# Sliding-window attention: the sum of each softmax row is formed by TensorE and applied to the output instead of to the weights

## The reference, cut to what matters

```
scores = einsum("bhncd,bhnkd->bhnck", qc, kc) * SCALE
scores = where(mask, scores, -inf)
attn = softmax(scores, axis=-1)
out = einsum("bhnck,bhnkd->bhncd", attn, vc)
return out.reshape(B, S, E) @ w_out.T
```

## Time and profile before

| | us |
|---|---|
| median of 3 runs | 731.71 |
| lowest and highest run | 730.83, 732.27 |
| the profiled execution, whole | 733.66 |
| its span, first to last instruction | 731.8 |
| PE, DVE, ACT, POOL busy | 653.5, 486.1, 435.4, 201.2 |

### The profile page before, as it was taken

The page is one execution under the profiler, slowest core; times in us unless marked ns, Lnnn a source line. Parts: engine busy times, 40 slices in busy tenths (PEclk is TensorE's granted clock), DMA queues, the critical chain, the costliest instruction groups (busy, mean ns, idle before and its releaser), DMA issues.

```text
span 731.8 us, 13912 instructions
## 1 busy us (share of the span) xinstructions
PE 653.5 (89%) x4832; PEld 535.8 (73%) x4833; DVE 486.1 (66%) x1091; ACT 435.4 (59%) x1124; POOL 201.2 (27%) x354
## 2 busy tenths in 40 slices
PE   7888788999998998978989999999978799999950
PEld 5666678999998998854567788888865388887840
DVE  2577676478488478458877856666556577777735
ACT  4997857357458358357878747465342366566612
POOL 2455421032000000010233434444126222222315
PEclk9999899999999999998999999999999999999985
DMA  8997000220220241410020000000195101111114
GB/s 287 387 326 223 1 1 1 91 91 1 91 91 0 91 124 83 134 39 1 1 87 1 2 1 2 1 1 1 64 428 200 58 30 52 49 50 50 51 59 135
DMA packets 32226, 62.03 MB, mean 85 GB/s; under 512 B 2500, under 2 KB 26824, under 8 KB 29928
## 3 DMA queue, kind: packets, MB, share of 16 engines
q1 hardware_dynamic: 30152, 56.04, 22.6%
q0 software_dynamic: 2016, 5.22, 2.0%
HBM read 45.80 MB, written 15.55 MB: 84 GB/s over the span
## 4 chain that ended last, share of the span: by engine, by line
PE 63%; ACT 15%; DVE 14%; DMA 3%; issue 3%; POOL 2%; SPq 1%; POOLq 0%; ACTq 0%; DVEq 0%
PE banks L1785 41%; PE bank L1785 22%; ACT arena L777 5%; DVE U_split L1254 4%; ACT U_split L796 2%; DVE mx L1208 1%; DVE arena L1345 1%; ACT arena L815 1%; DMA ys<-arena 1%; ACT arena L842 1%; DMA arena<-ys 1%; DMA cst<-in_cst 1%; DVE wabs L1368 1%; ACT xT L731 1%; ACT arena L951 1%
## 5 line engine op out<-in xcount | busy, mean ns | idle before, releaser
L1785 PE MATMUL banks<-U_split 128*128 128x512 f32 (+1 forms) x616 | 146.8, 350 | 6.1 <-DVE U_split L1254 4.0
L1785 PE MATMUL bank<-U_split 128*128 128x256 f32 (+1 forms) x864 | 112.1, 285 | 6.9 <-DVE U_split L1254 6.2
L1785 PEld LDWEIGHTS banks<-U_split 128*128 128x128 f32 x616 | 96.4, 190 | 23.8 <-issue 8.0
L1785 PEld LDWEIGHTS bank<-U_split 128*128 128x128 f32 x864 | 105.5, 189 | 10.8 <-DVE U_split L1254 6.5
L796 ACT ACTIVATE U_split<-arena 128x1024 fp32r (+6 forms) x122 | 96.9, 822 | 21.1 <-DVE arena L1345 9.4
L1785 PE MATMUL banks<-cst,arena 128*128 128x128 f32 (+1 forms) x594 | 90.5, 280 | 4.7 <-DMA arena<-xs 1.7
L1785 PE MATMUL banks<-arena 128*128 (+4 forms) x632 | 84.8, 382 | 3.3 <-DVE arena L1202 2.3
L1785 PEld LDWEIGHTS banks<-cst,arena 128*128 128x128 f32 (+1 forms) x594 | 69.9, 143 | 17.3 <-POOL arena L647 2.7
L571 POOL TENSOR_SCALAR rstd<-mv 128x1 f32<-128x1 f32 x38 | 10.7, 281 | 260.4 <-DVE mv L1186 236.4
L1785 PEld LDWEIGHTS banks<-arena 64*128 64x128 f32 (+3 forms) x632 | 61.3, 177 | 20.8 <-issue 7.5
L1044 ACT ACTIVATE arena<-banks,dmx 128x128 f32<-128x128 f32 (+1 forms) x128 | 52.9, 424 | 38.6 <-DVE dmx L1542 38.6
(11 more groups left out here) (239 smaller groups left out, 1180.1 us busy)
## 6 DMA issues: line engine op xcount, KB each, us to landing
arena<-in_w_exp SPq DMA_DIRECT2D x8, 1536.0 KB, 14.1
xs<-arena SPq DMA_DIRECT2D x8, 1032.0 KB, 13.8
arena<-in_ctxT SPq DMA_DIRECT2D x4, 1601.0 KB, 6.9
arena<-in_ctx SPq DMA_DIRECT2D x4, 1536.0 KB
arena<-in_w_f SPq DMA_DIRECT2D x3, 1024.0 KB, 11.5
arena<-xs SPq DMA_DIRECT2D x23, 129.0 KB, 2.0
w_x<-in_w_x SPq DMA_DIRECT2D x9, 256.0 KB, 7.0
arena<-in_w_oh SPq DMA_DIRECT2D x1, 2048.0 KB, 8.5
```

What stands on the lines that cost most here:

```text
L1785: return nc.tensor.matmul(o, w, x, start=start, stop=stop, **k)
```

## The change

Five things are changed, all in the first block and its neighbourhood.

1. The exponentials no longer keep a row sum (`accum_out` is gone); `rsum`, `rinv`, the reciprocal of 128x8 on DVE and the multiplication on POOL are gone. `a_transpose(n)` waits for the exponentials.
2. New on PE, `a_sums(n)`: eight products of the turned weights `PT` with constant columns (`halves`: ones in 16 of 32 columns), which give the row sums spread over the 16 output rows of each head, 128x128 per group. They go into free columns of PS[0] or PS[1] (in the last batch PS[6]). They stand ahead of `a_scores(n + 4)`; those of groups 12 to 15 stand after the loop's last scores.
3. New on DVE, `a_sum_inverse(n)`: the reciprocal of these 128x128 sums, from the bank into `oT`, in round n+4 between mask and max. `a_outT(b)` moves from ACT to DVE and multiplies PS[7] by `oT`. The scores of round n also wait for the inverse of round n-1.
4. `a_project_out(b-1)` moves on PE from behind the scores to behind the transposes of its round.
5. ACT copies the turned weights of three groups of four (i=0, 1, 2) instead of two, DVE those of one.

The counter `x_neg` is merged into `x_exp`, and the numbers of `const_set` move with the four new memsets of `halves`.

```diff
...
         def on_act(n):
 
-            return n % GROUPS in (1, 2)
+            return n % GROUPS != 3
...
-                pool.wait_ge(G["a_norm"], GROUPS * b + 1)
...
-                pool.wait_ge(G["a_rinv"], n + 1)
-                g.tensor_tensor(sm[:, n % 4, :, :], sm[:, n % 4, :, :],
-                                rinv[:, n % 4, :].unsqueeze(2).broadcast_to([P, H0F, P]), ALU.mult).then_inc(G["a_norm"], 1)
...
-                    a.activation(sm[:, n % 4, h, :], sm[:, n % 4, h, :], ACT.Exp, bias=mx[:, n % 4, h:h + 1],
-                                 accum_out=rsum[:, n % 4, h:h + 1]).then_inc(G["a_exp"], 1)
+                    a.activation(sm[:, n % 4, h, :], sm[:, n % 4, h, :], ACT.Exp,
+                                 bias=mx[:, n % 4, h:h + 1]).then_inc(G["a_exp"], 1)
...
-                    if b > 0:
-                        a_outT(b - 1)
...
+            def a_sum_inverse(n):
+                b, i = divmod(n, GROUPS)
+                f, t = divmod(i, TPB)
+                dve.wait_ge(G["a_z"], n + 1)
+                if i == 0 and b > 0:
+                    dve.wait_ge(G["a_y"], b)
+                v.reciprocal(oT[:, f, t * P:(t + 1) * P], sums_bank(n)).then_inc(G["a_zinv"], 1)
+
+            def a_outT(b):
+                dve.wait_ge(G["a_o"], b + 1)
+                dve.wait_ge(G["a_zinv"], GROUPS * (b + 1))
+                v.tensor_tensor(oT, PS[7][:, :].rearrange("p (k t) -> p k t", k=KT), oT, ALU.mult).then_inc(G["a_o_sb"], 1)
...
                 a_mask(n)
-                if n >= 1:
-                    a_rinv(n - 1)
+                if n >= 4:
+                    a_sum_inverse(n - 4)
                 a_max(n)
+                if i == 3 and b > 0:
+                    a_outT(b - 1)
...
+            dve.wait_ge(G["a_z"], NG - 1)
+            for n in range(NG - GROUPS, NG - 1):
+                a_sum_inverse(n)
             b_split_q(0)
             b_split_k(0)
             b_split_v(0)
             a_weightsT(NG - 1)
+            a_sum_inverse(NG - 1)
             for b in range(B):
+                if b == 0:
+                    a_outT(B - 1)
...
+            def a_sums(n):
+
+                b, i = divmod(n, GROUPS)
+                if n == 0:
+                    pe.wait_ge(G["const_set"], 8)
+                pe.wait_ge(*pt_done(n))
+                if b == B - 1:
+                    pe.wait_ge(G["xT_done"], B - 2)
+                    pe.wait_ge(G["a_zinv"], NG - GROUPS if n < NG - 1 else n)
+                o = sums_bank(n)
+                for j in range(2):
+                    for r in range(QUADS):
+                        ins = mm(o[r * D0P:(r + 1) * D0P, :], halves[:, j, :], PT[:, n % 2, 2 * r + j, :], start=j == 0, stop=j == 1,
+                                 tile_position=(0, r * D0P))
+                ins.then_inc(G["a_z"], 1)
+
...
                 if n > 0:
                     pe.wait_ge(G["a_add"], n)
+                if n >= 5:
+                    pe.wait_ge(G["a_zinv"], n - 4)
+                if n >= 4:
+                    a_sums(n - 4)
...
-                pe.wait_ge(G["a_norm"], n + 1)
+                pe.wait_ge(G["a_exp"], H0F * (n + 1))
...
-                if i == 3 and b > 0:
-                    a_project_out(b - 1)
...
                 if n >= 2:
                     a_transpose(n - 2)
+                if i == 3 and b > 0:
+                    a_project_out(b - 1)
...
```

More of the change, by code:

```diff
@@ L377, in build @@
             const_set ln_var ln_rstd ln_done xT_raw xT_done
-            a_q a_k a_v a_q_sb a_k_sb a_v_sb a_vmix a_s a_add a_max a_exp a_rinv a_norm
+            a_q a_k a_v a_q_sb a_k_sb a_v_sb a_vmix a_s a_add a_max a_exp a_z a_zinv
             a_pt a_pt_act a_pt_dve a_o a_o_sb a_y a_y_sb ld_rest
             b_q b_k b_v hi_part lo_part c_Thi c_Tlo c_Rhi c_Rlo wk_split b_s b_max b_exp b_t b_pt_hi b_pt b_o b_o_sb b_ot b_ot_sb b_y
-            x_k x_neg x_exp x_kf x_kf_hi x_kf_lo x_m1 x_m1_sb x_m1T x_m1T_sb x_kv x_kvbd
+            x_k x_exp x_kf x_kf_hi x_kf_lo x_m1 x_m1_sb x_m1T x_m1T_sb x_kv x_kvbd
             w_abs w_sum w_scale w_round w_tern
@@ L557, in _ @@
             g.memset(mhalf[:, :], -0.5).then_inc(G["const_set"], 1)
+            g.memset(halves[:, 0, 0:D0], 1.0).then_inc(G["const_set"], 1)
+            g.memset(halves[:, 0, D0:D0P], 0.0).then_inc(G["const_set"], 1)
+            g.memset(halves[:, 1, 0:D0], 0.0).then_inc(G["const_set"], 1)
+            g.memset(halves[:, 1, D0:D0P], 1.0).then_inc(G["const_set"], 1)
             pool.wait_ge(G["const_set"], 2)
@@ L757, in a_values @@
                              PS[6][:, :].rearrange("p (h c d) -> p h c d", c=2, d=D0), ACT.Copy).then_inc(G["a_v_sb"], 1)
-            def a_outT(b):
-                act.wait_ge(G["a_o"], b + 1)
-                if b > 0:
-                    act.wait_ge(G["a_y"], b)
-                a.activation(oT, PS[7][:, :].rearrange("p (k t) -> p k t", k=KT), ACT.Copy).then_inc(G["a_o_sb"], 1)
             def a_weightsT(n):
@@ L841, in x_exp @@
                 low = kf_lo[:, n % 3, 0:words]
-                a.activation(low, PS[KBANKS[c % 4]][:, 0:words], ACT.Relu, scale=-1.0).then_inc(G["x_neg"], 1)
-                act.wait_ge(G["x_neg"], n + 1)
+                a.activation(low, PS[KBANKS[c % 4]][:, 0:words], ACT.Relu, scale=-1.0).then_inc(G["x_exp"], 1)
+                act.wait_ge(G["x_exp"], 2 * n + 1)
                 a.activation(low, low, ACT.Exp, scale=-1.0).then_inc(G["x_exp"], 1)
@@ L876, in _ @@
                 if b == 0:
-                    a_outT(B - 1)
+                    act.wait_ge(G["a_o"], B)
                 x_exp(CP * b)
@@ L1026, in e_exp @@
                     act.wait_ge(G["e_qf"], b - 1)
-                a.activation(eq[:, b % 2, :], PS[QUERY_BANKS[b]][:, :], ACT.Relu, scale=-1.0).then_inc(G["x_neg"], 1)
-                act.wait_ge(G["x_neg"], CP * B + b + 1)
+                a.activation(eq[:, b % 2, :], PS[QUERY_BANKS[b]][:, :], ACT.Relu, scale=-1.0).then_inc(G["x_exp"], 1)
+                act.wait_ge(G["x_exp"], 2 * CP * B + b + 1)
                 a.activation(eq[:, b % 2, :], eq[:, b % 2, :], ACT.Exp, scale=-1.0).then_inc(G["e_exp"], 1)
@@ L1208, in a_max @@
                 v.tensor_reduce(mx[:, n % 4, :], sm[:, n % 4, :, :], AX, ALU.max, negate=True).then_inc(G["a_max"], 1)
-            def a_rinv(n):
-                dve.wait_ge(G["a_exp"], H0F * (n + 1))
-                v.reciprocal(rinv[:, n % 4, :], rsum[:, n % 4, :]).then_inc(G["a_rinv"], 1)
+            def a_sum_inverse(n):
+                b, i = divmod(n, GROUPS)
+                f, t = divmod(i, TPB)
+                dve.wait_ge(G["a_z"], n + 1)
[6 more added lines that the diff above has]
+                v.tensor_tensor(oT, PS[7][:, :].rearrange("p (k t) -> p k t", k=KT), oT, ALU.mult).then_inc(G["a_o_sb"], 1)
             def a_weightsT(n):
@@ L2116, in _ @@
                     to_xT(0, b - 2)
+                if n == NG:
+                    a_sums(n - 4)
                 if i == 0 and n > 0:
                     a_output(n - 4)
+                if n >= NG:
+                    a_sums(n - 3)
                 if n >= 3 and (n - 3) % GROUPS > 0:
```

20 lines of the change are left out of this document (11 added, 9 removed).

## The result

The changed kernel takes 739.19 us (median of 6 runs, 737.12 to 739.94), the kernel before beside it 731.99 us (6 runs, 729.4 to 734.74). The ratio is 1.0081, with a 95% interval of 1.0058 to 1.0104. The prediction said 738.7 us, with 731.5 to 743 as its range and a chance of 0.83 for slower. The profiled execution took 739.94 us with a span of 738.1 us, 6.3 us more than the span before.

A forecast was written before the change was run, and what follows sets the result against it. ACT was taken to bound the kernel, PE close behind. Full-clock stretches (about +4) and half clock (+3) on the profiled 733.66 us gave 740.7, or 738.7 us as a median; range 731.5 to 743.

The forecast's parts named there:

- ACT is late before, PE next: Kernel before, 11 to 96 us: row sums hang on ACT, busy 66.4 of 80.1 us; PE, busy 65.0, comes next.
- Exponentials, 1.6 us for eight: On ACT, eight exponentials without sums take 1.6 us instead of 3.1, saving ACT about 20 us of its 66.
- the two equations: Fit to ACT's copies from SBUF: 0.09 us per instruction plus 0.84 ns per column, giving 0.2 us for 128 columns.
- the first stretch: Scores of group 0 to those of 3: only the shorter exponentials act, -3.0 us.
- The inverse, 0.96 us: On DVE, a 128-column reciprocal takes 0.96 us from a slope of 6.3 ns per column; sixteen take 15.4 us.
- The projection rounds: Rounds n = 7, 11, 15: projection waits for DVE 3.83 us after scores; PE idles 1.5 to 3 us.
- The end: Scores of 15 to first cross scores: three inverses, 2.9 us, stand openly on the path; +3.5 us.
- The clock: PE drops to half clock behind gaps, about 1.5 us per stretch; two stretches taken, +3 us.
- A: Rival: PE's clock falls in all gaps, adding 5.5 to 8 us, taken as 742 us; chance 0.17.
- B: Rival: DVE's reciprocal is as cheap as other elementwise work, 0.3 us, taken as 732 us; chance 0.12.
- C: Rival: ACT was the only bound and PE runs dense, never waiting for multiplied outputs, 727 us; chance 0.06.
- D: Rival: ACT's exponentials keep their 390 ns pitch, so ACT gains nothing, 741.6 us; chance 0.05.

The follow-up runs named there:

- the experiment with the copy: The changed kernel with each reciprocal of the 128x128 sums replaced by a plain copy of the same size (computation altered); 731.30 us, ratio 0.9977.
- the kernel with the sums kept: The changed kernel with accum_out back on ACT's 128 exponentials, the sums read by nobody; 740.37 us, ratio 1.0114.
- the sums twice: The changed kernel with each group's eight sum products on PE issued twice, same result; 742.30 us, ratio 1.0171.
- the turned round: The changed kernel with projection rounds reordered: PE does sums, transposes, scores, projection; DVE does inverse and multiplication ahead of mask and maximum; 730.43 us, ratio 0.9970.
- the end mended: The turned round plus inverses of groups 12 and 13 ahead of the last ln_end, 14 behind the projections' low parts; 727.79 us, ratio 0.9943.
- the kernel with the outputs first: The changed kernel with a_outT ahead of a_max on DVE in the projection rounds; 733.24 us, ratio 1.0014.
- the kernel with the filler: The changed kernel with eight unused 128x128 products of ones on PE between the last projection and first cross scores; 738.12 us, ratio 1.0074.

## Why the prediction was right, point by point

The likeliest forecast was right in kind: ACT leaves the path, PE then waits for what stands behind DVE's long reciprocals, and the clock falls behind such gaps. That the number came within 0.5 us is in part luck, since two misses cancelled (under "The clock"). The term that was worked out wrongly is that of the exponentials.

**ACT is late before, PE next.** Right. Leaving out the sums alone in the kernel before gave 8 us; putting them back into the change cost only 1 to 2. But ACT was to lose about 20 us of its 66, and lost 10.0: the exponentials took more than predicted.

**Exponentials, 1.6 us for eight.** Wrong size: 2.37 us (14.04 to 16.41), 0.296 us each. The timeline of ACT after:

```profile
14.04 2.46 ACT L776 ACTIVATE arena<-arena,mx 128x128 f32<-128x128 f32 x8 [2.67 <-DVE mx L1205]
16.41 0.58 ACT L742 ACTIVATE arena<-bank 128x512 f32<-128x512 f32 x1
```

The step that failed is the comparison: "I take 1.6, since these copies too have no sum and a source in SBUF". The copies of the earlier trace rows take no operand with a value for each partition, and each exponential takes one, its `bias` (the negated maxima). What such an operand costs stands in rows of ACT that the prediction did not use. Here are two copies that have one (the keys, `scale=parity`, L752), then one that has none (the values, L761), each of 512 columns from a bank; an advance is read from the start of one row to the start of the next. Short copies without such an operand come last. All are lines of the timeline of ACT after.

```profile
20.86 1.26 ACT L752 ACTIVATE arena<-bank,cst 128x512 f32<-128x512 f32 x2
22.00 2.45 ACT L776 ACTIVATE arena<-arena,mx 128x128 f32<-128x128 f32 x8
...
28.51 0.59 ACT L761 ACTIVATE arena<-bank 128x512 f32<-128x512 f32 x1
28.99 2.46 ACT L776 ACTIVATE arena<-arena,mx 128x128 f32<-128x128 f32 x8
...
406.35 0.44 ACT L793 ACTIVATE U_split<-arena 128x256 fp32r<-128x256 f32 x1
406.65 0.40 ACT L930 ACTIVATE arena<-bank 128x256 f32<-128x256 f32 x1
406.92 0.31 ACT L931 ACTIVATE arena<-bank 128x128 f32<-128x128 f32 x1
407.07 0.53 ACT L1052 ACTIVATE arena<-banks 128x384 f32<-128x384 f32 x1
```

With the operand a copy advances by 0.57 us, without it by 0.48: 0.09 us more. The trace of before has the same two advances, 0.57 (twice from 40.74 us on) and 0.47 us (at 40.27). Added to the 0.20 us of the two equations this gives 0.29 us, and 0.296 was measured. That the instructions are short is not the reason: for 256 columns from SBUF the equations give 0.305 us, and the copy at 406.35 us advances by 0.30; one of 128 columns, from a bank, advances by 0.15. No run took the bias away from the exponentials, so this is read from rows and not tested.

The Trainium skill ("VectorE: DVE Perf Modes", "The TRN2 errata") gave the estimate of 0.29 us, and the measured pitch agrees with it, though its figure is for a copy and what was measured is an exponential with a bias. By that estimate the first stretch would have been -2.2, where -2.4 was measured.

**The inverse, 0.96 us.** Right: 0.947. From 32 columns to 128 it is 6.2 ns for each column, as it was 6.3 from 8 to 32. The estimate of 1.2 us that the prediction worked out from the repeat count of 8 in the Trainium skill ("VectorE: DVE Perf Modes", "First, the fixed hardware budget") was too high by 0.25; the measurement decides. And the experiment with the copy shows that the prediction hung on this term, as it said: 7.9 us with its clock.

**The projection rounds.** The gaps were 2.84, 1.31 and 2.46 us (predicted 3, 1.5 and 2.8), released by the multiplication each time. From the scores of 7 to those of 11 it took 23.82 us, of which 1.59 is half clock, so 22.2 against the 22.7 predicted.

**The end.** Three inverses between the splits, 2.5 us (99.64 to 102.13) instead of 2.9, since behind each other they advance by 0.83 to 0.87 us; PE waits 2.13 us. Timeline of DVE after:

```profile
96.02 3.70 DVE L1261 TENSOR_TENSOR U_split<-arena,U_split 128x1024 fp32r<-128x1024 f32 x4 [0.16 <-ACT U_split L793]
99.64 2.57 DVE L1213 RECIPROCAL arena<-bank 128x128 f32<-128x128 f32 x3
102.13 0.62 DVE L1336 SCALAR_TENSOR_TENSOR U_split<-banks,U_split 128x512 fp32r<-128x512 f32 x1
```

The stretch was +4.0, predicted +3.5, and 1.5 of it is the third projection at half clock. The last inverse and multiplication, costed at nothing, were covered: DVE waited 2.98 us ahead of them and 0.27 us for PE again behind them, ahead of its last maximum.

**The clock.** Right in kind, short in number for the profiled execution: three stretches of 1.5 to 1.6 us, 4.6 us, where I had taken two and 3 us. The number varies from one execution to another: with like gaps, the kernel with the sums kept had two such stretches and that with the sums twice had one. The steps at full clock add up to 6.8 - 4.6 = 2.2 us instead of 3.9. The two misses cancelled, which is luck: the total is right within 0.5 us, but its parts are so only within 1.7.

**Rivals.** A (the clock falls in all gaps) lies nearer to the profiled execution than the forecast's two stretches, though its 742 us did not come out. B is excluded by the 0.947 us and confirmed in its price by the copy. C, that PE runs dense, needs the multiplication off its path: the turned round does that, without a cheaper reciprocal, and reaches 730.4, and 727.8 with the end mended. I had tied C to the price of the reciprocal; it hung on the order. D fell.

## What to carry to other kernels

When a division is moved from a few columns to many, price it from the slope of the reciprocal's own rows, not from other elementwise work: here a slope near six times a copy's made the difference between 731.3 and 739.2 us. A new step on the second engine should be placed by who waits behind it; two reorderings of the same instructions gave back 11 us by the medians, 10 by the ratios. And where PE is made to wait for a result, look for work of its own (here the transposes) that can be put into the wait, since the gap costs its length and then, often, the clock. And when an instruction is priced from others, compare every operand: by the rows here, a bias with a value for each partition is worth near a third of an exponential.

## What the runs showed of the hardware that I had not expected

An exponential of 128 columns advances by 0.29 us without its sum and by 0.385 us with it, so keeping the sum costs 0.09 us, though its read is a record of 0.19 us. In the rows, an operand with a value for each partition goes with another 0.09 us (0.57 against 0.48 us for a copy of 512 columns from a bank). Plain copies from SBUF advance by 0.30, 0.52 and 0.95 us for 256, 512 and 1024 columns.

The granted clock does not follow the gap's length alone. Granted clock in three stretches of the change (the third last figure of a row), and in the matching ones of the kernel with the outputs first:

```profile
41.00:51.00 10.00, 8.39 (x95) 6.30 (x96) 6.26 (x12) 4.30 (x13) 1.57 (x4) 0.83 1.09 324
84.00:94.00 10.00, 7.31 (x101) 5.74 (x101) 4.88 (x11) 5.01 (x14) 2.09 (x7) 0.83 0.01 2
100.00:108.00 8.00, 5.87 (x48) 4.04 (x50) 5.08 (x7) 0.60 (x1) 0.00 (x0) 0.79 0.01 2
```

```profile
41.00:51.00 10.00, 8.37 (x128) 5.96 (x128) 7.82 (x15) 6.33 (x18) 1.57 (x4) 1.00 1.09 294
81.00:91.00 10.00, 8.05 (x112) 6.68 (x111) 6.07 (x14) 7.46 (x18) 2.16 (x7) 1.00 0.01 2
95.00:102.00 7.00, 4.88 (x65) 3.54 (x64) 5.55 (x8) 0.60 (x1) 0.00 (x0) 1.00 0.01 2
```

A gap of 2.12 us is followed by full clock here and by half clock in the change (2.13 us). The trace of before already had such a case, which the prediction's rival A passed over: the 12 cross products took 3.08 us behind a gap of 2.15 us. With the row sums kept, the first projection behind a gap of 2.84 us ran at full clock (1.99 us) and the third, behind 2.46, did not (3.56); with the sums issued twice it was the other way round (3.04 behind 2.90, 1.99 behind 2.46). Which of two like gaps loses the clock stays open. It is the likeliest reason that single executions of one kernel differ by 3 to 7 us. The clocks on record fit with that: of the ten executions of the kernel with the filler, the five from 735.36 to 738.06 us have a mean granted clock of 0.977 to 0.982, the five from 738.18 to 742.19 us one of 0.968 to 0.972. No run was made to show which is the cause.
